# A four-layer kernel on one core: scan weights made inside the recurrence, the first scan chunk's loads inside the norm, its products on other PSUM banks, the expert router in two halves

## What is computed

```python
x = x + row_attention(layernorm(x))            # 4 heads of 32 channels, within each of 128 rows, pair bias, mask
t = t + recurrence(layernorm(t))               # y = sigmoid(norm(x W') + y V') token after token
x = x + mamba(ln(x)) + flip(mamba(flip(ln(x))))  # selective scan, 128 inner channels, 16 states, both ways
t = t + experts(layernorm(t))                  # 8 experts, the two largest router shares, rescaled to sum to 1
```

```python
def _mamba(x, ...):                        # called once forwards and once on the flipped tokens
    xc, z = split(x @ in_w.T)
    xc = silu(conv4(xc) + conv_b)
    dt, Bm, Cm = split(xc @ x_w.T);  dt = softplus(dt @ dt_w.T + dt_b)
    h = exp(dt * A) * h + dt * Bm * xc;    y = sum(h * Cm) + xc * D     # token after token
    return (y * silu(z)) @ out_w.T
def _L1_ffn_ref(x, ...):
    router_probs = softmax(x @ router_w + router_b)
    top_p, top_i = top_k(router_probs, 2);  top_p = top_p / sum(top_p)
    return einsum(top_p, take(x @ expert_w + expert_b, top_i))
```

## Time and profile before

| | |
|---|---|
| median of 3 runs | 2569.32 us (2566.36 to 2575.73) |
| the profiled execution's own time | 2567.49 us |
| its span, first to last instruction | 2565.7 us |
| busy: PE, DVE, ACT, POOL | 2189.9, 2180.1, 1763.6, 2076.0 us |
| mean granted TensorE clock | 0.942 of full speed |
| attention's norm, PE | 7.5 to 66.1 us |
| scan weights | 568.6 to 574.3 us |
| norm of the scan | 574.7 to 615 us |
| first scan to last | 650 to 2353 us |
| router block | 2407.5 to 2434.1 us |
| expert groups | 2434.6 to 2563.3 us |

### The profile page before, as it was taken

The page is one execution under the profiler, slowest core; times in us unless marked ns, Lnnn a source line. Parts: engine busy times, 40 slices in busy tenths (PEclk is TensorE's granted clock), DMA queues, the critical chain, the costliest instruction groups (busy, mean ns, idle before and its releaser), DMA issues. The chain is left out here.

```text
span 2565.7 us, 37339 instructions
## 1 busy us (share of the span) xinstructions
PE 2189.9 (85%) x9229; PEld 1137.4 (44%) x9306; DVE 2180.1 (85%) x2229; ACT 1763.6 (69%) x3998; POOL 2076.0 (81%) x1330
## 2 busy tenths in 40 slices
PE   8899997774799888998899888899889898887597
PEld 8566665562344444444444433343333333333543
DVE  5577777434899999999999999999999999997766
ACT  4799997565788877887788855656556565553386
POOL 4355555203899999999999999999999999997389
PEclk7899998786899999999999999999999999999799
DMA  3000000003677676676667777777777777773032
GB/s 70 13 12 12 12 11 9 1 1 85 222 228 231 219 232 225 231 230 226 227 226 235 228 240 253 244 231 239 239 234 248 233 244 237 230 245 127 3 69 60
DMA packets 192553, 421.10 MB, mean 164 GB/s; under 512 B 66548, under 2 KB 95705, under 8 KB 192474
## 3 DMA queue, kind: packets, MB, share of 16 engines
q1 hardware_dynamic: 190938, 416.01, 51.6%
q10 hardware_dynamic: 1536, 4.20, 0.5%
HBM read 387.63 MB, written 24.12 MB: 160 GB/s over the span
## 5 line engine op out<-in xcount | busy, mean ns | idle before, releaser
L1574 POOL TENSOR_TENSOR s_hc<-s_h,s_cc 128x1024 f32<-128x1024 f32 x512 | 1202.6, 2370 | 51.0 <-PE s_py L1337 37.3
L1337 PE MATMUL s_py<-s_hc,ident 128*128 128x512 f32 x2048 | 979.3, 603 | 19.1 <-DVE s_yo L1620 19.1
L1657 DVE TENSOR_TENSOR_SCAN s_h<-s_dA,s_state,s_pu 128x1024 f32<-128x1024 f32 x330 | 770.3, 2342 | 27.7 <-PE s_pu L1315 4.7
L1337 PEld LDWEIGHTS s_py<-s_hc,ident 128*128 128x128 f32 x2048 | 385.9, 193 | 384.7 <-issue 312.0
L1490 ACT ACTIVATE s_dA<-s_dt,ss_A 128x1024 f32<-128x1024 f32 x352 | 401.6, 1142 | 9.1 <-ACT s_brow L1453 7.7
L1495 ACT ACTIVATE s_pu<-s_dt,ss_A 128x1024 f32<-128x1024 f32 x160 | 178.4, 1115 | 322.0 <-DVE s_h L1657 316.8
L1567 POOL TENSOR_TENSOR s_dbx<-s_dtx,s_bb 128x1024 f32<-128x1024 f32 x160 | 379.1, 2369 | 6.9 <-DMA s_bb<-rows_scratch 6.9
L1657 DVE TENSOR_TENSOR_SCAN s_h<-s_pu,s_state,s_dbx 128x1024 f32<-128x1024 f32 x150 | 350.2, 2335 | 22.3 <-ACT s_pu L1495 20.1
L1633 DVE TENSOR_TENSOR s_pu<-s_pu,s_dtx 128x1024 f32<-128x1024 f32 x288 | 349.0, 1212 | 14.9 <-PE s_pu L1324 12.5
L1324 PE MATMUL s_pu<-s_bcs,ss_sel 128*128 128x512 bf16 x499 | 159.6, 390 | 133.8 <-DVE s_h L1657 129.7
L591 POOL TENSOR_TENSOR ar_ex<-ar_ex,ar_rs 128x512 f32<-128x512 f32 x128 | 133.3, 1041 | 157.8 <-DVE ar_rs L540 157.7
(11 more groups left out here) (272 smaller groups left out, 3590.3 us busy)
## 6 DMA issues: line engine op xcount, KB each, us to landing
s_cc<-rows_scratch SPq DMA_DIRECT2D x512, 512.0 KB, 4.6
s_bb<-rows_scratch SPq DMA_DIRECT2D x160, 512.0 KB, 5.0
s_n<-n_scratch SPq DMA_DIRECT2D x64, 258.0 KB, 5.5
y_scratch<-s_yo SPq DMA_DIRECT2D x16, 512.0 KB, 5.4
s_yf<-y_scratch SPq DMA_DIRECT2D x16, 512.0 KB, 6.6
x_tok<-in_x_dram SPq DMA_DIRECT2D x16, 256.0 KB, 4.5
at_xg<-at_xT SPq DMA_DIRECT2D x64, 64.0 KB, 2.1
n_scratch<-ss_turned SPq DMA_DIRECT2D x32, 128.0 KB, 2.8
```

Of the source, the lines that this page charges most:

```text
L1337: ins = nc.tensor.matmul(p_y[:, hf], lhsT=c.ident[:, :], rhs=hc[:, s % RING, hf], start=(s == 0), stop=(s == U - 1))
L1574: nc.gpsimd.tensor_tensor(hc[:, s % RING, :], h[:, s % RING, :], cc[:, s % C_RING, :], ALU.mult).then_inc(read, 1)
L1657: nc.vector.tensor_tensor_scan(out=flow(h[:, s % RING, :]), data0=flow(decays), data1=flow(inputs), initial=begun, op0=ALU.mult, op1=ALU.a ...
```

## The change

- **Attention's norm:** the 48 matmuls ahead of it are gone, and its turning is a transpose. A new flag `plain` keeps the plain form for the experts' norm only.
- **Scan weights:** the block is gone. The eight DVE operations on the taps stand at the start of the recurrence's DVE list, the PE products behind its last step and before the convergence test, the DVE evacuations at the start of the block that adds to x, POOL's selector in the recurrence. Exp of A_log and its sign go to ACT's list in the scan's start (`decay_rates`).
- **Norm of the scan:** the two loads of chunk 0 are issued behind the stores of group 5 and those of chunk 1 behind group 6, when the groups they read have landed; the wait for all stores moves to the load of chunk 2. Six matmuls by the identity stand at the end of PE's list (`WAKE = 6`, another constant than the 48 before).
- **First chunk:** `run` takes a list `begin`. The rows of B and C go through `s_py`, the columns of B through `s_pu1`, so that the step size follows the convolution in `s_pp`.
- **Experts:** router and groups share one block. The router works on two halves of 64 rows; half 0 comes first, half 1's operations stand one by one (in two places two) between the groups 0 to 15, with its temporaries in PSUM. The expert ring has four banks instead of eight.

```diff
-                            if use is not None:
+                            if plain:
                                 ins = nc.tensor.matmul(bank[:, r * Q:(r + 1) * Q], lhsT=block_in, rhs=c.ident[:, :],
                                                        start=True, stop=True)
                             else:
...
+            if wake:
+                pe.wait_ge(taken, NCH - 3)
+                for _ in range(wake):
+                    nc.tensor.matmul(ps[:, 0, 0:Q], lhsT=c.ident[:, :], rhs=c.ident[:, :], start=True, stop=True)
...
             norm_stage(nc, c, "at_n", 1.0 + 1e-5, 1e-5 * 1e-6, evacuate, load=x_in, more_loads=load_weights,
-                       more_sets=set_constants, before=wake, use=pair)
...
+                pe.wait_ge(scaled, 8)
+                for way in range(2):
+                    for pair in range(2):
+                        nc.tensor.transpose(pw[:, 0, (2 * way + pair) * 128:(2 * way + pair + 1) * 128],
+                                            tp[:, way, pair, :, :].rearrange("p a d -> p (a d)"), c.ident[:, :])
+                nc.tensor.transpose(pw[0:D, 1, ZC], later.inz[:, :], c.ident[:, :])
+                nc.tensor.transpose(pw[:, 1, OC], later.ow[:, :], c.ident[0:D, 0:D])
+                nc.tensor.transpose(pw[:, 1, XC], later.xw[:, :], c.ident[0:RANK + BCW, 0:RANK + BCW])
+                nc.tensor.matmul(pw[:, 1, TC_], lhsT=later.xw[0:RANK, :], rhs=later.dtw[:, :], start=True,
+                                 stop=True).then_inc(later_turned, 1)
...
+            @block.gpsimd
+            def _(pool):
+                nc.gpsimd.memset(later.sel[:, :], 0.0).then_inc(cleared, 1)
+                nc.gpsimd.memset(later.zero[:, :], 0.0).then_inc(cleared, 1)
...
+                order = (((3, 2), (1, 0)), ((2, 3), (0, 1)))
+                for way in range(2):
+                    for pair in range(2):
+                        for half in range(2):
+                            tap = order[way][pair][half]
+                            nc.vector.tensor_scalar(tp[:, way, pair, half, :], later.inx[:, :], later.cw[:, tap:tap + 1],
+                                                    None, ALU.mult).then_inc(scaled, 1)
                 starts(shifted, 1, started)
...
+                dve.wait_ge(later_turned, 1)
+                for way in range(2):
+                    for pair in range(2):
+                        nc.vector.tensor_copy(later.taps[:, way, pair, :],
+                                              pw[:, 0, (2 * way + pair) * 128:(2 * way + pair + 1) * 128]
+                                              ).then_inc(later_copied, 1)
...
+WAKE = 6
...
+        def load_chunk(sp, m, at):
+
+            for half in range(2):
+                sp.dma_start(ns[half * D:(half + 1) * D, m % 2, :],
+                             nd[:, at + 1 - half:at + 1 - half + TC + 2 * PAD]).then_inc(n_loaded[m % 2], 16)
...
+                    if g == 5:
+                        sp.wait_ge(edged, 32)
+                        sp.wait_ge(kept[0], 32)
+                        sp.wait_ge(kept[1], 32)
+                        load_chunk(sp, 0, 0)
+                    if g == 6:
+                        sp.wait_ge(kept[2], 32)
+                        load_chunk(sp, 1, TC)
+            norm_stage(nc, c, "ss_n", 1.0, 1e-6, evacuate, keep=keep, wake=WAKE)
...
+            for step in begin:
...
 
             def step_size(hf):
                 def step(w, m, par):
-                    bc_taken(w, m)
+                    if at_start(m):
+                        pe.wait_ge(conv_taken, 1)
+                    else:
+                        bc_taken(w, m)
...
-                    ins = nc.tensor.matmul(p_p[0:BCW, hf], lhsT=k["bc"][:, :], rhs=xc[:, par, hf], start=True, stop=True)
+                    ins = nc.tensor.matmul((p_y if at_start(m) else p_p)[0:BCW, hf], lhsT=k["bc"][:, :], rhs=xc[:, par, hf], start=True, stop=True)
...
             def turn_x(w, m, par):
 
+                if at_start(m):
+                    pe.wait_ge(bt_taken, 1)
+                    pe.wait_ge(r_copied, 1)
                 pe.wait_ge(dtx_done, m + 1)
...
+            run(pe, unit, prepare.get, tail.get, own.get,
+                (convolve(a), convolve(b), step_size(a), step_size(b), in_out(a), in_out(b), columns_b, turn_x))
...
+            def decay_rates(w, m, par):
+                nc.scalar.activation(k["al"][:, :], k["al"][:, :], ACT.Exp).then_inc(rates, 1)
+                act.wait_ge(rates, 1)
+                nc.scalar.activation(k["A"][:, :], k["al"][:, :], ACT.Copy, scale=-1.0).then_inc(rates, 1)
+                act.wait_ge(rates, 2)
...
+            run(act, unit, prepare.get, tail.get, own.get,
+                (silu_x, softplus_relu, softplus_abs, bc_rows, softplus_exp, softplus_one, softplus_log, part_high,
+                 take_columns_b, part_middle, decay_rates, take_dt, take_turned_x))
             silu_z(backward, ALL - 1, 1)
...
             def load_n(m):
-                if m >= 2:
-                    sp.wait_ge(conv, m - 1)
+                if m == 2:
+                    for stored in n_kept:
+                        sp.wait_ge(stored, 16 * (NG // 4))
+                sp.wait_ge(conv, m - 1)
                 need(sp, z_made, m - NC - 1)
-                W_ = TC + 2 * PAD
-                for half in range(2):
-                    sp.dma_start(ns[half * D:(half + 1) * D, m % 2, :],
-                                 nd[:, base(m) + 1 - half:base(m) + 1 - half + W_]).then_inc(n_loaded[m % 2], 16)
+                load_chunk(sp, m, base(m))
...
+        match_0, rest_0 = sb("er_match", [Q, HALF_S, EXPERTS]), sb("er_rest", [Q, HALF_S, EXPERTS])
+        work = ctx.enter_context(nc.psum_tensor("er_work", [Q, 2, HALF_S, EXPERTS], F32))
+        match, rest = (match_0[:, :, :], work[:, 0, :, :]), (rest_0[:, :, :], work[:, 1, :, :])
+        key, tot = sb("er_key", [Q, S]), sb("er_tot", [Q, S])
...
+        ps = ctx.enter_context(nc.psum_tensor("ee_ps", [Q, GR, EXPERTS, D], F32))
...
+        @block.tensor
+        def _(pe):
+            def group(g, k, i):
+                pe.wait_ge(loaded[k], 32 * (i + 1))
+                for j in range(GR):
+                    need(pe, weighed, g * GR + j - GR + 1)
+                    nc.tensor.matmul(ps[:, j, :, :], lhsT=xg[:, k, j * Q:(j + 1) * Q], rhs=we[:, :, :],
+                                     start=True, stop=True).then_inc(made, 1)
+            pe.wait_ge(biased, 16)
+            pe.wait_ge(ranked, EXPERTS + 2)
+            for k in range(SLOTS):
+                group(k, k, 0)
+            with pe.Fori(1, NG // SLOTS) as i:
+                for k in range(SLOTS):
+                    group(SLOTS * i + k, k, i)
...
+            for a in range(2):
+                act.wait_ge(shifted, a + 1)
+                nc.scalar.activation(match[a], routes[:, part(a), :], ACT.Exp).then_inc(exped, 1)
+            for g in range(NG):
+                k = g % SLOTS
+                need(act, summed, g - SLOTS + 1)
+                nc.scalar.copy(hw[:, k, :, 0, :], c.x[:, g * GR:(g + 1) * GR, :]).then_inc(carried, 1)
+                if g % (NG // 2) == 0:
+                    act.wait_ge(weighted, g // (NG // 2) + 1)
...
+            def invert_sum(a, of):
+                chain(nc.vector.reduce_sum(tot[:, part(a)], of, AX.X))
+                chain(nc.vector.reciprocal(tot[:, part(a)], tot[:, part(a)]))
+
+            def share(a):
+                chain(nc.vector.tensor_tensor(routes[:, part(a), :], match[a], wide(tot[:, part(a)]), ALU.mult))
+
+            def largest(a, of):
+                chain(nc.vector.reduce_max(key[:, part(a)], of, AX.X))
...
+            def first_of(a, pick):
+                chain(nc.vector.tensor_tensor(pick, match[a], wide(key[:, part(a)]), ALU.is_equal))
+
+            def leave_out(a):
+                chain(nc.vector.scalar_tensor_tensor(out=rest[a], in0=e[:, part(a), :], scalar=-2.0,
+                                                     in1=routes[:, part(a), :], op0=ALU.mult, op1=ALU.add))
...
+            shift(0)
+            shift(1)
             dve.wait_ge(exped, 1)
-            chain(nc.vector.reduce_sum(tot[:, :], e[:, :, :], AX.X))
-            chain(nc.vector.reciprocal(tot[:, :], tot[:, :]))
-            chain(nc.vector.tensor_tensor(p[:, :, :], e[:, :, :], wide(tot[:, :]), ALU.mult))
...
+            weights(0)
+            group(0, 0, False)
+            dve.wait_ge(exped, 2)
+            invert_sum(1, match[1])
+            group(1, 1, False)
+            share(1)
+            group(2, 2, True)
+            largest(1, routes[:, part(1), :])
+            group(3, 3, True)
+            equal(1, routes[:, part(1), :])
...
+            invert_sum(1, match[1])
+            group(14, 2, True)
+            weights(1)
+            group(15, 3, True)
```

389 lines of the change are left out of this document (169 added, 220 removed).

## The result

| | before | after |
|---|---|---|
| median | 2569.75 us (4 runs, 2566.36 to 2575.73) | 2530.12 us (4 runs, 2526.23 to 2533.66) |
| profiled execution's own time | 2567.49 us | 2533.66 us |
| its span | 2565.7 us | 2531.9 us |

The ratio is 0.9843 (95% interval 0.9819 to 0.9867). A second series gave 0.9834 (0.9821 to 0.9848): 2528.70 us of 5 runs against 2570.81 of 9. The forecast was 2530. The medians lie 39.6 us apart, the two profiled executions 33.8. Between their landmarks the 33.8 divide as follows; each line is the difference of two stretches, measured from the end of the one ahead.

The account below looks back on a forecast made before the run. GpSimd busiest in the scan, left unchanged; the waits ending last at stage seams were costed. Gains 4.2 + 6.1 + 7.7 + 1.4 + 3.8 + 15.0 = 38.2 off 2567.5 give 2529.3, forecast 2530 us, range 2518 to 2543.

Parts of the forecast that it names:

- Attention's norm: Attention's norm: TensorE at 1.2 GHz throughout, 2.63 us a chunk, last pair at 61.9; gain 4.2 us (1.9 to 6.8).
- Rival 1: Attention's norm: TensorE at 2.4 GHz, VectorE's pace governs; gain 14.9 us, total 2519; chance 0.12.
- Scan weights: Between recurrence and scan's norm: the block goes, its work covered by idle VectorE and TensorE; gain 6.1 us (5.3 to 6.6).
- First loads: Before the first convolution: loads issued beside the norm, convolution 0.54 us behind the stores; gain 7.7 us (5 to 8).
- made good after four chunks: Scan's norm: SyncE, with 0.7 us free a chunk, makes up 2.4 us of load issue in four chunks.
- three chunks in hand: Scan's norm: ACT, refilling slots when the store of four chunks before has landed, has three chunks to spare meanwhile.
- rival 3: Scan's norm: SyncE falls behind, ACT waits for slots; of 7.7 us remain 3, total 2534; chance 0.07.
- Clock of the first convolution: First convolution: six matmuls ahead let it take 3.7 us or less instead of 5.12; gain 1.4 us (0 to 1.7).
- if these count as the convolution's own first 3 us did: First convolution: condition that the six matmuls (2.6 us) raise TensorE's clock, giving 3.7 us or less.
- First chunk: Scan's first chunk: step size starts 5.3 us earlier, ACT's row copy and transfer issue take back 1.4; gain 3.8 us.
- Experts: Experts: half 0 ends at 2423.8, GpSimd starts 17.6 us earlier, then 3.65 a group; gain 15.0 us (6.5 to 16.5).
- Rival 2: Experts: router steps stretch beside GpSimd and hold groups up; gain 6.5 us instead of 15.0, total 2538; chance 0.15.

Follow-up runs that it names:

- second series: The changed kernel as it is, once more, five runs against the kernel before: 2528.70 us, ratio 0.9834 (0.9821 to 0.9848).
- all eight executions: Profiles of the changed kernel (twice) and six variants that issue the six matmuls and load early: convolution 3.67 us in five, 5.37 in three.

## Why the prediction was right, and where only by balance

The time, 2530, was met within a microsecond, the sum for the profiled execution (2529.3) missed 2533.7 by 4.4. The mechanisms held in the main, but so close a hit is luck: four of the six terms were off by 1 us or more, the four runs lie between 2526.23 and 2533.66, and the second series gave 2528.70. Point by point:

- *Attention's norm*, 4.2 forecast, 6.2 measured. The mechanism was right (1.2 GHz throughout, TensorE's own pace from its third chunk). Mis-sized was the period: 2.63, "the middle", where it is 2.45, near the low end that the earlier trace rows allows. And the kernel before is not fixed at 66.14; with 72.15 the same change gives 12 us. There the clock fell at about 27 us, so its fall does not hang on the long centring at 31.51 that the prediction tells it by. Rival 1 (2.4 GHz) did not occur, and with the 48 matmuls back it still did not. The plain form raises the clock here and transposes do not. The Trainium skill ("TensorE: Matmul & The Clock Gate", Part 4, on PE-mode transpose) says that transposes do not count as busy for the clock in the same way; the traces agree, with a rise at 24 us against none in this norm.
- *Scan weights*, 6.1 forecast, 5.6 in the trace, 6.1 when undone. Right, with the cover as named; 0.5 came back as idle time of VectorE ahead of the scan's norm.
- *First loads*, 7.7 forecast, 6.7 measured, 6.2 when undone. The step "made good after four chunks" held: the stores of group 10 begin where they did before. What failed is the step that gave ACT "three chunks in hand": the stores landed in 4.2 us instead of 2.8, ACT waited 2.5 us for them in all, and the last store ended 0.8 us later against the norm's start (38.33 against 37.54; 37.56 again with the loads behind the stores). The rest is the change of block, 0.70 where I had 0.54. This is rival 3 (loads and stores collide) at a small size, 0.8 of the 4.7 us that it was priced at.
- *Clock of the first convolution*, 1.4 forecast, -0.25 in the profiled execution, 1.45 in five others. The step "if these count as the convolution's own first 3 us did" holds so far: the clock rose during the six matmuls in all eight executions. I had left out the idle time between them and the convolution: 0.59 to 1.80 us in the five, 1.86 to 2.01 in the three that took 5.37. Measured against the matmuls' absence (6.31) they are worth 0.9 or 2.6.
- *First chunk*, 3.8 forecast, 3.8 measured, 3.9 when undone. The kernel before varies here too: 26.32 in the execution with four banks.
- *Experts*, 15.0 forecast, 17.0 measured. Half 0's chain took 16.1 us where I had 16.3, and GpSimd's first addition came after 19.3 us where I had 20.0. The second group is 5.0 behind the first where I had 5.6 (4.9 to 6.0 in the variants, 5.6 in the changed kernel again), and nothing was lost later, for which I had taken off 0.6. Rival 2 was the right danger in the wrong place: with SBUF temporaries it costs 3.1, in PSUM nothing. Its price of 8.5 was too high by its own numbers, since it counts both the stretch (16 x 0.35) and the overrun that the stretch makes (16 x 0.2); with 0.25 a group free, 0.35 overruns by 0.1. The Trainium skill ("SBUF — State Buffer", section "SBUF: two separate sides") names two SBUF inputs as a condition; the traces agree, with 0.69 grown to 1.79 in the one case and unchanged in the other.
- *Scan*, 0 forecast, -5.8 in the profiled execution. It is variation: the same kernel again took 5.1 us less there. The medians lie 39.6 apart where the sum says 38.2 (42.1 in the second series).

What balanced: attention's norm and the experts brought 4 us more than forecast in the profiled execution, their norm 0.9 (it varies from 39.46 to 40.28 in the variants), loads, weights and the convolution 3.2 less.

## What to carry to other kernels

Cost a change at the seams of a kernel stage by stage, from the wait that ends last in each, and measure it the same way afterwards: here single terms were good to 2 us while whole executions differed by 7. Work moved beside a GpSimd-bound stretch stayed free here, where it fits the slack per group and its temporaries are in PSUM. Loads moved ahead of stores can make the stores land later, so look at who waits for a landing and not only at the queue that issues. Matmuls that are to have TensorE's clock up should end close to the work they serve (gaps of 0.30 to 1.80 us were fast here, 1.86 to 2.01 slow), and replacing plain identity matmuls by transposes cost the fast clock here and still won, by half the turning passes.

## What the runs showed of the hardware

- Behind plain fp32 matmuls by the identity the clock rose: 5.9 us after the first in attention's norm with the plain form. Four transposes and eight 8-column products per chunk did not raise it in 30 us of TensorE at 5.00 of 5.00 busy (25 to 55 us in the changed kernel). Once fast, idle gaps of 1.26 (before), 0.70 (before with four banks), 0.64 (plain form), 1.30 and 0.46 (48 matmuls) stood next to its fall.
- The clock column shows 1.00 before the first change of clock, with passes of 0.21 us.
- Between the matmuls at the end of the scan's norm and the convolution, idle gaps of 0.30 (28 passes ahead), 0.90 (20), and 0.59, 1.09, 1.17, 1.24 and 1.80 us (12) were followed by a convolution of 3.67 us, gaps of 1.86, 2.01 and 2.01 us (12) by one of 5.37, and a gap of 7.73 by one of 6.31.
- With four loads of 258 KB issued between them, stores of 128 KB landed in 4.2 us (median) instead of 2.8.
- VectorE with two SBUF inputs and GpSimd stretch each other: 0.69 to 1.79 and 2.35 to 2.80; 0.42 to 1.24. Each time the length added is 0.14 us short of what the operation that had begun first still had to run: 1.10 of 1.24, 0.45 of 0.59, 0.82 of 0.96.
